# Attention and a tiled feed-forward on one core: weights placed beside x, sums on GpSimd, low-rank factors from the preamble, row-tiled low-rank products

## The chip, the cores and the metric

One core of one Trainium2 chip runs the whole program. The metric is the device time of one launch in microseconds. TensorE (PE; its weight loads are PEld), VectorE (DVE), ScalarE (ACT), GpSimd (POOL) and SyncE (SP, which only issues DMAs) each run their own list of instructions in order and wait for one another through semaphores.

## What is computed

T = 2048 tokens of 512 features; 128 heads of 4 content and 64 rope features; a feed-forward with 1376 hidden rows. `tile` repeats a matrix of 128 columns four times.

```python
def _L0_attn_ref(x, Wq_down, Wq_up, Wq_rope, Wkv_down, Wk_up, Wv_up, Wk_rope, Wo):
    ...
    scores = (jnp.einsum('bqhd,bkhd->bhqk', q_c, k_c) + jnp.einsum('bqhd,bkd->bhqk', q_r, k_r)) / scale
    attn = jax.nn.softmax(scores, axis=-1)
    out = jnp.einsum('bhqk,bkhd->bqhd', attn, v_c)
    ...
    return out @ Wo
def _qlora_linear(x, wq, A, B):
    w = jnp.tile(wq, (1, 4))
    return x @ w.T + x @ A.T @ B.T * 0.5
def _L0_ffn_ref(x, ...):
    gate = jax.nn.silu(_qlora_linear(x, w1q, a1, b1))
    up = _qlora_linear(x, w3q, a3, b3)
    return _qlora_linear(gate * up, w2q, a2, b2)
xn = _layernorm(x, axis=-1)
s = attention(xn)
g = _silu(_L0_ffn_ref(xn, ...))
return x + s * g
```

## The kernel before

**Precision.** A float32 product is made of three passes of reduced operands: high by high, low by high and high by low. ScalarE copies a value to the reduced type (the high part, names in `h`), and VectorE or GpSimd subtracts it from the original (the low part, names in `l`). A product written with plain float32 operands takes one instruction in the program, but the trace counts two or more passes for it.

**Preamble** (`project_inputs`, 0 to 77 us). It normalises x, transposes it into `xh` and `xl` (4 blocks of 128 features by 2048 tokens each, resident to the end), and projects it by the columns of `ws`: 128 columns of latents, 64 of the key's rope part (`kp`, rows 0 to 63) and the same 64 once more, whose high part ScalarE puts in `krlh` rows 64 to 127. What SyncE stores last ends it.

**Attention** (`attention`, 77 to 1805 us). `groups` runs `body` of each engine over 16 groups of 16 steps, in a rolled loop; the last group is unrolled. A step projects one block of queries (`project`), makes row scores by query block for the maxima (`row_scores`), and two steps later the scores with keys in the rows (`scores`), the exponentials, and the values. For each pair of steps VectorE's maxima are transposed and laid by a SyncE DMA (`max_rows`, `slot<-mrow`) into the row of the operand that subtracts them; the scores wait for it. In the unrolled last group, each engine runs `tail(eng, k)` of `finish` behind `body(at, k)`, for steps k = 0 to 22 (16 and above finish what the first 16 began). SyncE's order in a step is contents (`slot<-kc`, `k<-kc`), maxima row, values, stores of the outputs.

**Feed-forward** (`finish`). Since `tile` repeats the weights, x can be summed over its four blocks first: `sums` has TensorE multiply `xh` and `xl` by ones-on-the-diagonal (`oner`), 8 products for each of four chunks of 512 tokens, in the tail at k = 17 and 19; the results are split into `sh` and `sl`. `lora` then makes the low-rank products x A of all chunks (`lah`, `lal`: the factors three times over), 48 products, split into `lr`. A chunk (`tensor_rest`, `chunk`) has 12 column tiles of hidden rows (three row ranges `FR` = 128, 128, 88 of each of four blocks of 344): each tile makes `gp` and `up` from 3 weight products and 1 low-rank product (`b13` by `lr`, 96 rows) each, L1384 to L1387. ScalarE applies Silu, VectorE multiplies (`hid`, L1268), adds the blocks (`hsum`, L1280) and splits the sum; after tiles 5 and 9 and after the loop `low_rank` (L1355) multiplies `hid` by `a2` into `zp`, four products in four column strips. Beside it the attention output of the chunk is loaded (`num`, `den`), VectorE takes reciprocals of `den` (L1245, one for each of four feature blocks, in the y stage), GpSimd multiplies (`normalise`, L1098), and both parts of the result go to `attn_out` (L1369, 12 products for 128 tokens). The y stage makes for each 128 tokens 9 products of hidden sums by `w2h`, `w2l` (L1409) and one of `z` by `b2` in float32 (L1411), applies Silu, multiplies by the attention output and adds x. In chunk 0, `weights_hi` splits w2 and Wo between the tiles. Chunks 1 and 2 run in a rolled loop.

## Time and profile before

| | us |
|---|---|
| median of the runs (2024.77 to 2025.87) | 2024.78 |
| the profiled execution | 2028.5 |
| its span | 2026.4 |
| TensorE busy | 1984.1 |
| VectorE busy | 1411.8 |
| ScalarE busy | 1060.0 |
| GpSimd busy | 468.2 |
| chain that ended last: TensorE's share | 93% |

The profiled execution is one launch; its span is from the first to the last instruction of the trace, and all times in the rows below are in it. Busy times of engines overlap. Matmuls are pipelined, so the difference between two starts, and not a row's duration, is what one costs. A matmul in float32 shows as x2 or more.

### The profile page before, as it was taken

The numbers are of one execution on the slowest core, as the hardware profiler recorded it, in microseconds if no ns is written. First come the engines' busy times: TensorE is split into PE (matmuls) and PEld (weight loads), VectorE is DVE, ScalarE is ACT, GpSimd is POOL, SyncE is SP. The second block draws the span as 40 slices with busy tenths as digits, with TensorE's granted clock in tenths as the row PEclk, the third lists the DMA queues.
The fourth block names the chain that finished last, engine by engine and source line by source line (L and its number), as shares of the span: only waits on it lengthen the run. The fifth ranks groups of instructions, "written<-read, shape, count | busy, mean of one in ns | idle before, by whom it ended". The sixth has DMA issues, their size and how long they took to land.

```text
span 2026.4 us, 38967 instructions
## 1 busy us (share of the span) xinstructions
PE 1984.1 (98%) x12576; PEld 1532.0 (76%) x12576; DVE 1411.8 (70%) x1619; ACT 1060.0 (52%) x1539; POOL 468.2 (23%) x771
## 2 busy tenths in 40 slices
PE   7799999999999999999999999999999999988998
PEld 5577777777777777777777777777777777866776
DVE  7667667677676676776767767667677676767664
ACT  5355555555555555555555555555555555553222
POOL 2112121212222222212121212121212222114221
PEclk9899999999999999999999999999999999999999
DMA  7412121211112121212121212111111112122221
GB/s 253 149 28 43 34 40 38 39 35 38 39 32 44 28 47 29 49 28 48 26 49 28 49 29 42 33 39 38 39 35 38 39 32 63 26 77 89 84 83 47
DMA packets 128856, 102.69 MB, mean 51 GB/s; under 512 B 51510, under 2 KB 94518, under 8 KB 128814
## 3 DMA queue, kind: packets, MB, share of 16 engines
q1 hardware_dynamic: 128814, 102.15, 21.5%
q8 instruction: 24, 0.39, 0.1%
q14 instruction: 18, 0.15, 0.0%
HBM read 50.71 MB, written 25.17 MB: 37 GB/s over the span
## 4 chain that ended last, share of the span: by engine, by line
PE 93%; DVE 2%; ACT 1%; issue 1%; POOLq 0%; ACTq 0%; DVEq 0%
PE pj L879 35%; PE st L849 24%; PE sx L866 12%; PE ob L826 12%; PE ap L1369 2%; PE sx L834 1%; PE zp L1409 1%; PE yp L1409 1%; PE gp L1384 1%; PE zp L1355 1%; PE up L1387 0%; PE gp L1387 0%; PE up L1386 0%; PE gp L1385 0%; PE up L1384 0%
## 5 line engine op out<-in xcount | busy, mean ns | idle before, releaser
L785 DVE TENSOR_REDUCE mx<-sx 128x4 f32<-128x1024 f32 x512 | 627.0, 1225 | 452.9 <-PE sx L866 434.8
L766 ACT ACTIVATE probs<-st 128x1024 f32<-128x1024 f32 x512 | 512.7, 1026 | 166.6 <-PE st L849 166.6
L736 ACT ACTIVATE slot<-pj 64x512 fp32r<-64x512 f32 x512 | 303.9, 594 | 443.5 <-PE pj L879 437.2
L849 PE MATMUL st<-slot,k 89*128 89x512 f32 x1024 | 417.8, 408 | 1.2 <-ACT probs L766 1.2
L686 POOL CAST k<-kc 64x512 fp32r<-64x512 f32 x256 | 167.4, 654 | 1060.4 <-PE st L849 1060.1
L849 PE MATMUL st<-slot,krlh 128*128 128x512 f32 x1024 | 406.9, 397 | 0.0
L879 PE MATMUL pj<-xh,wh 128*128 128x512 f32 x1024 | 402.6, 393 | 4.0 <-PEq L216 3.0
L879 PE MATMUL pj<-xh,wl 128*128 128x512 f32 x1024 | 402.2, 393 | 0.0
L879 PE MATMUL pj<-xl,wh 128*128 128x512 f32 x1024 | 402.0, 393 | 0.0
L795 DVE TENSOR_TENSOR slot<-pj,slot 64x512 fp32r<-64x512 f32 x512 | 352.7, 689 | 16.3 <-ACT slot L736 0.3
L866 PEld LDWEIGHTS sx<-k,slot 88*128 88x128 f32 x2048 | 306.8, 190 | 66.8 <-issue 28.4
L866 PE MATMUL sx<-k,slot 88*128 88x256 f32 x2048 | 335.4, 286 | 4.4 <-DVE mx L785 2.7
L826 PE MATMUL ob<-probs,vx 128*32 128x256 f32 x4096 | 247.6, 382 | 0.0
L879 PEld LDWEIGHTS pj<-xh,wh 128*128 128x128 f32 x1024 | 193.9, 189 | 42.4 <-issue 5.0
L879 PEld LDWEIGHTS pj<-xh,wl 128*128 128x128 f32 x1024 | 193.5, 189 | 42.0
L879 PEld LDWEIGHTS pj<-xl,wh 128*128 128x128 f32 x1024 | 193.8, 189 | 38.0
L849 PEld LDWEIGHTS st<-slot,k 89*128 89x128 f32 x1024 | 195.6, 191 | 30.5 <-issue 2.2
L849 PEld LDWEIGHTS st<-slot,krlh 128*128 128x128 f32 x1024 | 195.1, 191 | 29.4
L826 PEld LDWEIGHTS ob<-probs,vx 128*32 128x32 f32 x4096 | 120.0, 109 | 83.4 <-issue 0.4
L799 DVE CAST slot<-slot 64x1024 fp32r<-64x1024 f32 x256 | 176.0, 688 | 7.9
L719 POOL TENSOR_TENSOR wl<-w_stage,wh 128x512 fp32r<-128x512 f32 x60 | 77.0, 1283 | 59.1 <-ACT wh L771 59.1
L747 ACT ACTIVATE mrow<-sx 16x128 fp32r<-16x128 f32 x128 | 33.3, 260 | 86.1 <-PE sx L834 86.1
(168 smaller groups left out, 1405.5 us busy)
## 6 DMA issues: line engine op xcount, KB each, us to landing
w_stage<-in_Wq_rope SPq DMA_DIRECT2D x64, 256.0 KB, 3.0
c_scratch<-stage SPq DMA_DIRECT2D x32, 256.0 KB, 2.9
c_in<-c_scratch SPq DMA_DIRECT2D x128, 64.0 KB, 1.9
o_scratch<-o_sb SPq DMA_DIRECT2D x128, 64.0 KB, 2.1
k<-kc SPq DMA_DIRECT2D x128, 48.0 KB
slot<-kc SPq DMA_DIRECT2D x256, 24.0 KB
k<-kx SPq DMA_DIRECT2D x128, 48.0 KB
slot<-kx SPq DMA_DIRECT2D x256, 24.0 KB
```

The lines of the kernel that those rows point to most:

```text
L686: nc.gpsimd.tensor_copy(k1[0:64, s, :, :].rearrange("p a n -> p (a n)"), krh[:, bp * CH:(bp + 1) * CH]).then_inc(k_ready, 1)
L719: nc.gpsimd.tensor_tensor(wl[:, s], w_stage[:, s % 2], wh[:, s], ALU.subtract).then_inc(w_ready, 1)
L736: nc.scalar.activation(slot1[0:64, (k - 1) % NS, e, :, :], pj[64 * e:64 * e + 64, :].rearrange("p (a n) -> p a n", a=2), ACT.Copy).then_in ...
L766: nc.scalar.activation(probs[:, k % NS, kt], st[:, kt], ACT.Exp, scale=SCALE).then_inc(exp_done, 1)
L785: nc.vector.tensor_reduce(mx[:, p, lo:lo + 4], sx[:, :, :].rearrange("p a (b k) -> p (a b) k", b=2), axis=AX.X, op=ALU.max).then_inc(red_d ...
L795: nc.vector.tensor_tensor(slot2[64:128, s, e, :, :], pj[64 * e:64 * e + 64, :].rearrange("p (a n) -> p a n", a=2), slot1[0:64, s, e, :, :] ...
L799: nc.vector.tensor_copy(slot2[0:64, s], slot1[0:64, s]).then_inc(s2_done, 1)
L826: last = nc.tensor.matmul(ob[j:j + 32, 0, :], vx[:, s, 2 * h + kt, e, :], probs[:, s, kt, h, e * S:(e + 1) * S], start=(s == 0 and kt == 0 ...
L849: last = nc.tensor.matmul(st[:, kt, h, :].rearrange("p (e n) -> p e n", e=PH), kk, q[0:n_rows, s, :, h, :], start=(n == 0), stop=(n == 1))
L866: last = nc.tensor.matmul(sx[:, h, qt * S:(qt + 1) * S], slot1[0:KC, s, half, h, qt * 128:qt * 128 + 128], k1[0:KC, s, h, :], start=True, ...
L879: last = nc.tensor.matmul(pj[:, :], w[:, s, c, :], xx[:, c, ts], start=(c == 0 and n == 0), stop=(c == KD - 1 and n == 2))
L1369: last = nc.tensor.matmul(ap[i % 2][:, :], o[:, k, i * 128:(i + 1) * 128], w[:, k, :], start=(k == 0 and n == 0), stop=(k == KD - 1 and n ...
```

## The change

**Preamble.** The second copy of the key's 64 columns in `ws` gives way to the low-rank factors: `a1T` and `a3T` are loaded, GpSimd clears the columns and copies the factors in six times, so that rows 64 to 127 of `kp` hold x A; ScalarE puts them in `lora_raw`. ScalarE splits `ws` in two pieces. What was the second copy now comes by a DMA from `krh` to `krlh` in each chunk.

**Tail of the last group.** The sums over the four blocks of x are made by GpSimd in float32, 28 additions, at most two in a step (k below 16). The weights are loaded into the space of x's low parts of groups that are done (`x_raw`, which shares memory with `xl`), and their high and low parts into slices of `xh` and `xl`; ScalarE and VectorE split them between the steps. The low-rank factors b come in 42 DMAs of two partitions at k = 2; masks (`mk`, made at k = 0) choose for each partition whether it holds the high or the low part, so that 12 rows of one operand carry all three terms. Half of the reciprocals are taken at k = 15 and 16, on `den1`, which holds the denominator of each head once and is spread to its rows through a scratch in memory by broadcast DMAs.

**Feed-forward.** No sums and no low-rank products stand ahead of it. 11 column tiles replace 12: the remainders of 88 rows carry a piece of the fourth block in rows 96 and up (a second VectorE product in these tiles). A tile has six `wide` products and two `narrow` ones (rows 32g to 32g + 11 of `b13` and of `lora`, in one of four row strips by `tile_position`). The narrow ones of two tiles stand together. `z` by `b2` is one reduced product whose rows carry three terms (`zh` by ScalarE, `zt` and `z` by VectorE). One reciprocal in a chunk stands behind column tile 7. TensorE's chunks are unrolled.

```diff
-            sp.dma_start(ws[:, :, 192:256], wk_rope.rearrange("(k p) n -> p k n", p=128)).then_inc(small_loaded, 16)
+            for n, a in enumerate((a1T, a3T)):
+                sp.dma_start(a_raw[:, :, RANK * n:RANK * (n + 1)],
+                             a.rearrange("(k p) n -> p k n", p=128)).then_inc(a_loaded, 16)
...
+                sp.wait_ge(krh_done, c + 1)
+                sp.dma_start(krlh[64:128, c * CH:(c + 1) * CH].bitcast(F32),
+                             krh[:, c * CH:(c + 1) * CH].bitcast(F32)).then_inc(krh_copied, 16)
...
+            nc.gpsimd.memset(ws[:, :, 192:256], 0.0).then_inc(a_zero, 1)
+            pool.wait_ge(a_zero, 1)
+            pool.wait_ge(a_loaded, 32)
+            for g in range(2):
+                for n in range(3):
+                    lo = 192 + 32 * g + 2 * RANK * n
+                    nc.gpsimd.tensor_copy(ws[:, :, lo:lo + 2 * RANK], a_raw[:, :, :]).then_inc(a_copied, 1)
+            pool.wait_ge(ws_hi, 2)
...
-                nc.scalar.activation(krlh[64:128, xs], kp[64:128, :], ACT.Copy).then_inc(krh_done, 1)
+                nc.scalar.activation(lora_raw[:, xs], kp[64:128, :], ACT.Copy).then_inc(lora_done, 1)
...
-            act.wait_ge(small_loaded, 64)
-            nc.scalar.activation(wsh[:, :, :], ws[:, :, :], ACT.Copy).then_inc(ws_hi, 1)
+            act.wait_ge(small_loaded, 48)
+            nc.scalar.activation(wsh[:, :, 0:128], ws[:, :, 0:128], ACT.Copy).then_inc(ws_hi, 1)
             for i in range(NTL):
                 hi_transposed(0, i)
+                if i == 1:
+                    act.wait_ge(a_copied, 6)
+                    nc.scalar.activation(wsh[:, :, 128:256], ws[:, :, 128:256], ACT.Copy).then_inc(ws_hi, 1)
...
+    def spread_den(sp):
+
+        for kt in range(KD):
+            sp.dma_start(den[:, kt, :], r_dram[32 * kt:32 * kt + 32, :].unsqueeze(1).broadcast_to([32, HD, CH])
+                         ).then_inc(den_spread, 16)
...
     def sync_tail(sp, k):
-        if k == 5:
...
-        if k == 16:
+        if k == 2:
+            sp.wait_ge(b_zero, 1)
+            for g in range(4):
+                w, half = g // 2, g % 2
+                for n in range(3):
+                    r = 32 * g + 4 * n + 2 * w
+                    for jj in range(2):
+                        j = 2 * jj + half
+                        src = (b1T, b3T)[w]
+                        if j < 3:
+                            sp.dma_start(b13_raw[r:r + RANK, jj * 384:jj * 384 + FB],
+                                         src[:, j * FB:(j + 1) * FB]).then_inc(b_loaded, 16)
+                            sp.dma_start(b13_raw[r:r + RANK, jj * 384 + 352:jj * 384 + 352 + PIECE[j]],
+                                         src[:, 3 * FB + 256 + 32 * j:3 * FB + 256 + 32 * j + PIECE[j]]).then_inc(b_loaded, 16)
+                        else:
+                            sp.dma_start(b13_raw[r:r + RANK, jj * 384:jj * 384 + 256],
+                                         src[:, j * FB:j * FB + 256]).then_inc(b_loaded, 16)
...
+        if k == 13:
+            sp.wait_ge(at_sems.proj_done, projected(11))
+            sp.wait_ge(s_step, 21)
+            sp.dma_start(wo_raw, wo.rearrange("(k p) n -> p k n", p=128)).then_inc(wo_loaded, 16)
+        if k == 17:
             for landed in at_sems.ct_in:
                 sp.wait_ge(landed, 48 * NT)
-            sp.wait_ge(at_sems.o_stored, 32 * (NT - 2))
-            load_attention(sp, o_dram, den, 1, 0, den_loaded)
...
+        if k == 18:
+            sp.wait_ge(ab2_zero, 2)
+            sp.wait_ge(r_stored, 16)
+            spread_den(sp)
+            load_num(sp, 0)
+            sp.dma_start(w2_raw[:, 0:2, :], w2qT[0:256, :].rearrange("(k p) n -> p k n", p=128)).then_inc(w2_loaded, 16)
+            sp.dma_start(w2_raw[0:FR[2], 2, :], w2qT[256:FB, :]).then_inc(w2_loaded, 16)
+            for r in range(NR):
+                sp.dma_start(a2[0:FR[r], r, :, 0:RANK],
+                             a2T.rearrange("(j p) n -> p j n", j=4)[128 * r:128 * r + FR[r], :, :]).then_inc(a2_loaded, 16)
+            for j in range(4):
+                for n in range(3):
+                    sp.dma_start(b2_raw[32 * j + RANK * n:32 * j + RANK * (n + 1), :], b2T).then_inc(b2_loaded, 16)
 
...
     def pool_tail(pool, k):
...
+        if k == 1:
+            nc.gpsimd.memset(b13_raw[:, :], 0.0).then_inc(b_zero, 1)
+        if k < 16:
+            cs = slice(c * CH, (c + 1) * CH)
+            terms = [xx[:, kt, cs] for kt in range(KD) for xx in (xh, xl)]
+            for n in range(2 * (k % 4), min(2 * (k % 4) + 2, 7)):
+                if n:
+                    pool.wait_ge(s_step, 7 * c + n)
+                nc.gpsimd.tensor_tensor(s_raw[:, cs], s_raw[:, cs] if n else terms[0], terms[n + 1],
+                                        ALU.add).then_inc(s_step, 1)
+        if k in (4, 8):
+            w = c - 1
+            pool.wait_ge(at_sems.proj_done, projected(4 * w + 3))
+            pool.wait_ge(s_step, 7 * w + 7)
+            nc.gpsimd.memset(x_raw[:, :, w * CH + FB:w * CH + 384], 0.0).then_inc(pad_zero, 1)
+        if k == 16:
+            pool.wait_ge(at_sems.proj_done, projected(15))
+            pool.wait_ge(s_step, 28)
+            nc.gpsimd.memset(a2[:, :, :, :], 0.0).then_inc(ab2_zero, 1)
+            nc.gpsimd.memset(b2_raw, 0.0).then_inc(ab2_zero, 1)
...
     def act_tail(act, k):
...
+        if k in (4, 6, 8):
+            i = k // 2 - 2
+            act.wait_ge(b_loaded, 16 * 42)
+            wait(act, b_done, i)
+            nc.scalar.activation(b13_hi[:, :], b13_raw[:, 256 * i:256 * i + 256], ACT.Copy, scale=0.5).then_inc(b_hi_done, 1)
...
     def vector_tail(dve, k):
...
+        if k in (6, 10, 14, 18):
+            c = k // 4 - 1
+            cs = slice(c * CH, (c + 1) * CH)
+            dve.wait_ge(sh_done, c + 1)
+            nc.vector.tensor_tensor(sl[:, cs], s_raw[:, cs], sh[:, cs], ALU.subtract).then_inc(sl_done, 1)
...
+        if k in (15, 16):
+            n = k - 15
+            dve.wait_ge(den_loaded, 16)
+            nc.vector.reciprocal(den1[:, 256 * n:256 * n + 256], den1[:, 256 * n:256 * n + 256]).then_inc(recip, 1)
...
                     wait(dve, zmm_done, c * NR + max(r - 1, 0))
-                nc.vector.tensor_tensor(hid[0:n, r % 2, j, :], up[m % 2][0:n, :], gate[0:n, m % 2, :],
-                                        ALU.mult).then_inc(hid_done, 1)
+                product = nc.vector.tensor_tensor(hid[0:n, r % 2, j, :], up[m % 2][0:n, :], gate[0:n, m % 2, :], ALU.mult)
+                if r == 2:
+                    lo = 32 * j
+                    product = nc.vector.tensor_tensor(hid[lo:lo + PIECE[j], 0, 3, :], up[m % 2][96:96 + PIECE[j], :],
+                                                      gate[96:96 + PIECE[j], m % 2, :], ALU.mult)
+                product.then_inc(hid_done, 1)
                 if j == 1 and r > 0:
                     lo_part(c, r - 1)
...
                                             ALU.subtract).then_inc(ol_done, 1)
+                if m == 7 and more:
+                    dve.wait_ge(den_loaded, 16 * (c + 2))
+                    nc.vector.reciprocal(den1[:, :], den1[:, :]).then_inc(recip, 1)
...
+            add_block(c, 2, 3)
+            lo_part(c, 2)
+            dve.wait_ge(zh_done, c + 1)
+            wait(dve, z_done, c)
+            nc.vector.tensor_scalar(zt[:, :], zp[:, :], mk[:, 4:5], None, ALU.mult).then_inc(zt_done, 1)
+            dve.wait_ge(zt_done, c + 1)
+            wait(dve, y_done, c * NI)
+            nc.vector.scalar_tensor_tensor(out=z[:, :], in0=zh[:, :], scalar=mk[:, 5:6], in1=zt[:, :],
+                                           op0=ALU.mult, op1=ALU.add).then_inc(z_done, 1)
             for i in range(NI):
...
     def tensor_tail(pe, k):
-        if k == 17:
-            pe.wait_ge(la_hi, 1)
-            pe.wait_ge(at_sems.ql_done, 2 * NS * NT)
-            sums(pe, 0)
-            pe.wait_ge(at_sems.red_done, 2 * NS * NT)
-            sums(pe, 1)
-        if k == 19:
-            pe.wait_ge(at_sems.mrow_ready, NS * NT // 2)
-            sums(pe, 2)
...
-            sums(pe, 3)
-
...
     def tensor_rest(pe):
-        def lora(c):
-            if c < NC - 1:
-                pe.wait_ge(sl_done, c + 2)
-            else:
-                pe.wait_ge(lr_done, 1)
-            for k in range(KD):
-                for n, (w, xx) in enumerate(((lah, xh), (lah, xl), (lal, xh))):
-                    last = nc.tensor.matmul(tb[(NC + c) % 3][0:96, :], w[:, k, :], xx[:, k, c * CH:(c + 1) * CH],
-                                            start=(k == 0 and n == 0), stop=(k == KD - 1 and n == 2))
-            last.then_inc(lp_done, 1)
...
+            def wide(m):
+
+                r, j = m // 4, m % 4
+                for w, (dst, done) in enumerate(banks):
+                    wide_h, wide_l = (x[:, j, w * CH + 128 * r:w * CH + 128 * r + 128] for x in (xh, xl))
+                    nc.tensor.matmul(dst[m % 2][:, :], wide_h, sh[:, cs], start=(m % 2 == 0), stop=False)
+                    nc.tensor.matmul(dst[m % 2][:, :], wide_h, sl[:, cs], start=False, stop=False)
+                    last = nc.tensor.matmul(dst[m % 2][:, :], wide_l, sh[:, cs], start=False, stop=(m % 2 == 1))
+                    if m % 2:
+                        last.then_inc(done, 1)
+
+            def narrow(m):
+
+                r, j = m // 4, m % 4
+                for w, (dst, done) in enumerate(banks):
+                    row = 32 * (2 * w + j % 2)
+                    lo = 384 * (j // 2) + 128 * r
+                    last = nc.tensor.matmul(dst[m % 2][:, :], b13[row:row + LR, lo:lo + 128], lora[row:row + LR, cs],
+                                            start=(m % 2 == 1), stop=(m % 2 == 0), tile_position=(row, 0))
+                    if m % 2 == 0:
+                        last.then_inc(done, 1)
+
+            def bank_free(m):
+                if m >= 2:
+                    pe.wait_ge(hid_done, c * MT + m - 1)
+                else:
+                    wait(pe, hid_done, c * MT)
...
+            for m in range(0, MT, 2):
+                bank_free(m)
+                wide(m)
+                if m + 1 < MT:
+                    bank_free(m + 1)
+                narrow(m)
+                if m + 1 < MT:
+                    narrow(m + 1)
+                    wide(m + 1)
+                if m in (4, 8):
+                    low_rank(m // 4 - 1)
...
                         nc.tensor.matmul(yp[i % 2][:, :], h[0:n, r, ts], w[0:n, r, :],
                                          start=(r == 0 and q == 0), stop=False)
-                nc.tensor.matmul(yp[i % 2][:, :], z[:, ts], b2[:, :], start=False, stop=True).then_inc(y_done, 1)
```

Three places of the order in which the engines run.

SyncE, in the last group around step 2 (`slot1<-mrow`: the row of maxima; `k1<-kc`, `slot1<-kc`: contents). Before:

```order
L622 DMA slot1<-kc 12x1x512 x2
L618 DMA k1<-kc 24x1x512
L622 DMA slot1<-kc 12x1x512 x2
L653 DMA o_scratch<-o_sb 64x256 x2
L628 DMA slot1<-mrow 1x16x128
L618 DMA k1<-kc 24x1x512
```

Now, with 38 further DMAs of the same kind, two partitions each, where "..." stands:

```order
L647 DMA slot1<-kc 12x1x512 x2
L678 DMA o_scratch<-o_sb 64x256 x2
L1074 DMA b13_raw<-in_b1T 2x344
L1076 DMA b13_raw<-in_b1T 2x32
...
L1076 DMA b13_raw<-in_b3T 2x32
L1079 DMA b13_raw<-in_b3T 2x256
L653 DMA slot1<-mrow 1x16x128
L643 DMA k1<-kc 24x1x512
L647 DMA slot1<-kc 12x1x512 x2
```

42 DMAs of the factors b now stand between the store of an output and the row of maxima of step 0, and so ahead of the contents of step 3 too.

TensorE, the first column tiles of a chunk (`gp`, `up`: the banks of gate and up; 0 and 1 alternate with the tiles). Before:

```order
L1384 MATMUL gp0<-sh,w13h 128x512
L1385 MATMUL gp0<-sl,w13h 128x512
L1386 MATMUL gp0<-sh,w13l 128x512
L1387 MATMUL gp0<-lr,b13 128x512
L1384 MATMUL up0<-sh,w13h 128x512
L1385 MATMUL up0<-sl,w13h 128x512
L1386 MATMUL up0<-sh,w13l 128x512
L1387 MATMUL up0<-lr,b13 128x512
L1384 MATMUL gp1<-sh,w13h 128x512
```

Now (`kx` is the memory of `lora`):

```order
L1427 MATMUL gp0<-sh,xh 128x512
L1428 MATMUL gp0<-sl,xh 128x512
L1429 MATMUL gp0<-sh,xl 128x512
L1427 MATMUL up0<-sh,xh 128x512
L1428 MATMUL up0<-sl,xh 128x512
L1429 MATMUL up0<-sh,xl 128x512
L1439 MATMUL gp0<-kx,b13 128x512
L1439 MATMUL up0<-kx,b13 128x512
L1439 MATMUL gp1<-kx,b13 128x512
L1439 MATMUL up1<-kx,b13 128x512
L1427 MATMUL gp1<-sh,xh 128x512
L1428 MATMUL gp1<-sl,xh 128x512
```

The two low-rank products of each tile have moved out of its eight and stand with those of the next tile, four in a row.

VectorE, from column tile 7 on in a chunk with a next one. Before (its four reciprocals stand further on, in the y stage):

```order
L1268 TENSOR_TENSOR hid<-up1,gate 128x512
L1276 REGISTER_ALU
L1280 TENSOR_TENSOR hsum<-hsum,hid 128x512
L1264 REGISTER_ALU
L1268 TENSOR_TENSOR hid<-up0,gate 88x512
L1264 REGISTER_ALU
L1268 TENSOR_TENSOR hid<-up1,gate 88x512
```

Now:

```order
L1372 TENSOR_TENSOR hid<-up1,gate 128x512
L1345 REGISTER_ALU
L1349 TENSOR_TENSOR hsum<-hsum,hid 128x512
L1389 ISA
L1390 RECIPROCAL den1<-den1 128x512
L1368 REGISTER_ALU
L1372 TENSOR_TENSOR hid<-up0,gate 88x512
L1375 TENSOR_TENSOR hid<-up0,gate 32x512
L1368 REGISTER_ALU
L1372 TENSOR_TENSOR hid<-up1,gate 88x512
L1375 TENSOR_TENSOR hid<-up1,gate 32x512
```

The reciprocal stands ahead of the products of tiles 8 and 9, which have each become two, and the y stage keeps none.

## Rows read from the trace of the kernel before

**Rows 1.** Busy line of the page: busy us, share of the span, instructions.

```profile
PE 1984.1 (98%) x12576; PEld 1532.0 (76%) x12576; DVE 1411.8 (70%) x1619; ACT 1060.0 (52%) x1539; POOL 468.2 (23%) x771
```

**Rows 2.** Stretches: us, length, busy us (x instructions) of PE, PEld, DVE, ACT, POOL; PEclk, DMA share, GB/s.

```profile
150.00:1780.00 1630.00, 1630.00 (x10917) 1274.11 (x10916) 1147.43 (x1287) 902.77 (x1285) 377.28 (x681) 1.00 0.19 38
1874.90:1923.49 48.59, 48.59 (x214) 34.59 (x212) 34.26 (x36) 14.14 (x24) 10.16 (x9) 1.00 0.26 87
1817.44:1874.90 57.46, 49.20 (x214) 34.33 (x212) 41.98 (x37) 20.75 (x32) 26.74 (x16) 1.00 0.32 99
76.00:82.00 6.00, 5.22 (x12) 3.80 (x12) 4.23 (x5) 0.00 (x0) 3.63 (x7) 0.50 0.50 161
```

**Rows 3.** Chain that ended last, two chunks' first output products: start us, us, what.

```profile
1903.72 2.95 PE ap L1369 x12
...
1952.31 2.95 PE ap L1369 x12
```

**Rows 4.** Timeline of PE: start us, us, engine, line, operation, out<-in, count.

```profile
1882.52 0.40 PE L1384 MATMUL gp<-sh,w13h 128*128 x1
...
1884.39 0.39 PE L1384 MATMUL gp<-sh,w13h 128*128 x1
...
1886.04 0.39 PE L1387 MATMUL up<-lr,b 96*128 x1
1886.35 1.06 PE L1355 MATMUL zp<-hid,a 128*32 128x512 f32 x8
1887.35 0.51 PE L1384 MATMUL gp<-sh,w13h 128*128 x1
1887.69 0.40 PE L1385 MATMUL gp<-sl,w13h 128*128 x1
```

**Rows 5.** Timeline of PE in the y stage.

```profile
1868.57 1.02 PE L1411 MATMUL yp<-b,z 128*128 128x512 f32 x2
...
1869.66 0.39 PE L1369 MATMUL ap<-wol,xh 128*128 128x512 f32 x1
```

**Rows 6.** Timeline of GpSimd and VectorE in chunk 0.

```profile
1830.50 2.85 POOL L1123 TENSOR_TENSOR w2l<-raw,w2h 128x1024 fp32r<-128x1024 f32 x1
...
1831.02 2.89 DVE L1285 TENSOR_TENSOR xl<-num,xh 128x512 fp32r<-128x512 f32 x1
...
1833.83 0.68 DVE L1268 TENSOR_TENSOR hid<-up,gate 128x512 f32<-128x512 f32 x1
...
1854.23 3.34 DVE L1245 RECIPROCAL den<-den 128x512 f32<-128x512 f32 x1
```

**Rows 7.** Timeline of PE, from the first low-rank product to the first gate product.

```profile
1804.74 0.48 PE L1338 MATMUL tb<-xh,lah 128*96 128x512 f32 x1
...
1817.44 0.39 PE L1384 MATMUL gp<-sh,w13h 128*128 128x512 f32 x1
```

**Rows 8.** Issues of DMAs: count, KB each, us to landing.

```profile
slot<-mrow SPq DMA_DIRECT2D x128, 8.0 KB, 1.8
```

**Rows 9.** Groups of the page: count, busy us, mean ns, idle before and releaser.

```profile
L785 DVE TENSOR_REDUCE mx<-sx 128x4 f32<-128x1024 f32 x512 | 627.0, 1225 | 452.9 <-PE sx L866 434.8
...
L766 ACT ACTIVATE probs<-st 128x1024 f32<-128x1024 f32 x512 | 512.7, 1026 | 166.6 <-PE st L849 166.6
...
L719 POOL TENSOR_TENSOR wl<-w_stage,wh 128x512 fp32r<-128x512 f32 x60 | 77.0, 1283 | 59.1 <-ACT wh L771 59.1
```

**Rows 10.** Timeline of SyncE's queue in the last group.

```profile
1691.43 1.19 SPq L653 DMA_DIRECT2D o_scratch<-o_sb  x2
1696.38 0.57 SPq L628 DMA_DIRECT2D slot<-mrow  x1
...
1801.14 0.25 SPq L1025 DMA_DIRECT2D rawb<-in_b1T  x1
1801.44 0.25 SPq L1026 DMA_DIRECT2D rawb<-in_b3T  x1
```

**Rows 11.** Timeline of PE: the first score that needs the row of maxima.

```profile
1700.45 0.40 PE L849 MATMUL st<-slot,k 89*128 89x512 f32 x1
```

**Rows 12.** The loads of a2: duration ns min/median/max, first and last start.

```profile
L1038 SPq DMA_DIRECT2D a<-in_a2T x3: 390/508/3020, 1814.3 to 1815.3; - x3
```

506 lines of the change are left out of this document (240 added, 266 removed).

## The prediction, as recorded before the result

> **What bounds the kernel now.** I read the page's busy line first, then stretches of time, then the instructions inside them. TensorE is busy 98% of the span [rows 1], and through the attention (150 to 1780 us) it is busy every microsecond at a granted clock of 1.00 [rows 2]: there only TensorE's work counts, and everything else has room until it makes TensorE wait. The edit changes that program in its last sixteen steps alone, and what comes behind. The feed-forward has four chunks of 512 tokens. The steady ones repeat every 48.59 us (attention-output products at 1903.72 and at 1952.31, [rows 3]) with TensorE busy for all 48.59 us and VectorE for 34.26 [rows 2]. The first chunk takes 57.46 us, 8.9 more, TensorE being busy for only 49.20 of them [rows 2]. So the end is TensorE's count of products plus whatever makes it wait.
>
> **The products, chunk by chunk.** A column tile (eight products) starts at 1882.52 and the next at 1884.39: 1.87 us, 0.2335 a product [rows 4]. Twelve tiles make 22.4 us. The new loop has 11 tiles with six wide products each, 66 x 0.2335 = 15.4 us, and six groups of "narrow" products (12 rows in one of four row strips). No row shows a row-strip product. Its bounds: free concurrency and no changeover, 0.23 us a group; four in series, 0.93. The nearest row is the low-rank group, four f32 products in four column strips. From 1886.27 (where the next product would have stood) to 1887.35, plus the 0.11 by which the next spacing (0.34) is long [rows 4], it costs 1.19 us, while one f32 product alone costs 1869.66 - 1868.57 - 0.23 = 0.86 [rows 5]. So a group costs one product plus 0.33 of changeover: I take 0.23 + 0.33 = 0.56, six times 3.4. The loop's products fall from 22.4 to 18.8, by 3.6. The y products: the last of ten (z by b2) was f32 at 0.86 and becomes a single pass at 0.23, four times 0.63 = 2.5. TensorE's floor in a chunk is 48.6 - 3.6 - 2.5 = 42.5 us.
>
> The Trainium skill (TensorE: Matmul & The Clock Gate, Measured speedup vs the span model) has four row tiles at 3.07 times, and (TensorEngine Tiling (Array Packing), Key Properties) says that changing the tiling mode drains the engine. By the first alone a group would be 0.30 us and the four chunks some 6 us shorter; by the second there is a changeover on top, and the low-rank rows [rows 4] agree with it.
>
> **VectorE becomes the limit inside the loop.** Its 32 short operations of a steady chunk average (34.26 - 4 x 3.34)/32 = 0.65 us [rows 2, 6]. Of the four reciprocals one is left, but it moves from the y stage into the loop, behind column tile 7. From the end of tile 7 VectorE does product, add, reciprocal 3.34, then the two parts of product 8: 0.2 + 4 x 0.67 + 3.34 = 6.2 us. TensorE needs product 8 for tile 10, and until there has 1.4 (wide 8) + 0.56 + 1.4 (wide 9) + 1.2 (low rank) = 4.5: it waits some 1.8. Tiles 3 to 6 hold twelve VectorE operations (7.8 us) against 6.7 us of TensorE, and part of that arrears, 0.5, comes out at tile 8. So chunks 1 and 2 take 42.5 + 2.3 = 44.8; the last one has no reciprocal, 42.5 + 0.3 = 42.8. Gains: 3.8, 3.8 and 5.8. The z chain (ScalarE, then two VectorE operations in a row, about 2.5 us) lies beside twelve attention-output products (2.73 us) and costs nothing by a hair; if that cover were gone it would be 0.5 a chunk.
>
> Chunk 0 loses its wait for the b factors (8.9 over the steady length, before) but has new work on the same queues: w2's low part, b2's two masking operations, and on ScalarE a wait for twelve b2 loads queued behind 2.7 MB (1.0 of spread denominators, 1.0 of outputs, 0.7 of w2). The extra lies between 0 and the old 8.9; I take 3.4: chunk 0 is 48.2, a gain of 9.3.
>
> **From the end of attention to the first tile.** The 48 low-rank products and their wait, 1804.74 to 1817.44, go: 12.7 us [rows 7]. The 32 sum products go, two blocks of 16 x 0.2335 = 3.7 us; they covered waits. The first block lay over the landing of the row of maxima (1.8 us [rows 8]), the second over an exponential (1.03 us [rows 9]) and its handoffs. I let 3.1 of the 7.5 come back as waiting, between 0 and 7.5. GpSimd's sums end two steps earlier and the weights' splitting at step 18, so nothing later is due; VectorE's second half-reciprocal pushes the last maxima by under 1 us, which is in the 3.1. Gain 17.1.
>
> **What is added in the attention's last group.** (a) SyncE: 42 DMAs at step 2, each of two partitions. Two in a row of this kind start 0.295 us apart [rows 10], so they hold the queue for 12.4 us. Behind them stands the row of maxima for step 0 and the contents of step 3. In the old order the queue is idle from 1692.62 to 1696.38, 3.8 us, and the maxima land at 1696.38 + 1.8 = 1698.2, needed at 1700.45 [rows 8, 10, 11]. So TensorE stops for 12.4 - 3.8 - 2.2 = 6.4 us, and 0.6 more for the contents two DMAs further: 7.0. Nothing hides it, as every score waits for that row. After a pause of this size the clock may fall: at 76 to 82 us the clock reads 0.50, the lower level of 1.2 GHz, behind waits at the end of the preamble [rows 2], where twelve products at half the clock cost 12 x 0.23 = 2.8 us more; in chunk 0, with 8.3 us of pauses, it stayed 1.00. I take 1.5. (b) VectorE's, ScalarE's and GpSimd's extra pieces. VectorE idles before the first maxima of each step (452.9 us over 256 steps, 1.8 each [rows 9]), and the pieces are up to 2.8 us (step 6). GpSimd adds 28 sums of 1.28 us, two a step (the 128x512 difference in [rows 9]). Such an instruction can hold up a VectorE operation with two SBUF inputs: in chunk 0 the difference, whose kind takes 0.68 us, that starts at 1831.02 took 2.89 and ended 0.6 after GpSimd's 1830.50 + 2.85 [rows 6]. Few of VectorE's operations in the steps have two SBUF inputs, so I take 1.0 for the sixteen steps, bounds 0 and 20 (below). (c) Preamble: two small loads, a later split of half the weights, a 64-partition copy per chunk on SyncE, whose queue ends the preamble: 0.5.
>
> **Sum.** -9.3 -3.8 -3.8 -5.8 -17.1 + 7.0 + 1.5 + 1.0 + 0.5 = -29.8. The profiled execution took 2028.5 (span 2026.4); the median of the runs is 2024.8, and the same difference is taken off it: **1995 us**.
>
> **Rivals.**
> A. The 42 DMAs do not stop TensorE, since they may issue faster when nothing else is queued: without 7.0 + 1.5 it is 1986.5. Against it: the rows of such DMAs agree within 0.01. 12%.
> B. The strips do not overlap or cost two changeovers, 0.93 instead of 0.56: 6 x 0.37 = 2.2 less a part hidden by the VectorE waits, about 1.8 a chunk, and chunk 0 keeps 3 more: 2005. 17%.
> C. GpSimd's sums hold VectorE in each of the sixteen steps for one instruction, 1.28 us, with no room left: 16 x 1.28 = 20, 2015. For it: the 2.89 us row. Against it: VectorE's casts and maxima stood beside GpSimd's work unchanged so far. 11%. The Trainium skill (GPSIMD Engine Reference, Specifications) says that GpSimd contends with VectorE operations that have two SBUF inputs or run in a 2-port mode; the second half of that would add the casts of the steps to those held, and is what C would need.
> D. Slower than before: a two-partition DMA costs not 0.3 but 1.2 us at step 2. The stop is then 42 x 1.2 - 5.4 = 45 us, 2024.8 - 38.3 + 45 + 1.5 = 2033. It decides from 1.0 us a DMA, (38.3 - 1.5 + 5.4)/42. For it: one a2 load took 3.02 us to issue [rows 12], behind outputs and w2, 1.7 MB; against it, step 2 has next to nothing queued. 5%.
> E. The end is set elsewhere by a new wait of some 30 us that I don't see: no change, 3%.
> The forecast keeps 52%.
>
> **How the numbers follow.** The range takes in A, B and the unknowns of the forecast (chunk 0 by -3 to +5, the sums by 3) and most of C's way: 1983 to 2011, leaving out C's upper part, D and E. About 0.2% is what a measurement can tell from no change. Faster 0.92, same 0.03, slower 0.05.
>
> **What would show it.** One pause of TensorE of about 7 us near 1700, waiting for the maxima's row; the first gate product near 1810 (1817.4 - 17.1 + 10.0), with no low-rank product ahead of it; chunk starts 48, then 45 and 45 apart; in each of the first three chunks a wait of about 2 us on the product of tile 8 behind the reciprocal; four narrow products starting within 0.1 us of each other. It would be wrong if the steps with sums are longer than 6.7 us throughout, or the narrow products start 0.23 apart.

## The result

The changed kernel takes 2012.9 us (median of four, 2012.7 to 2014.1) against 2025.0 for the kernel before on the same chip: a ratio of 0.994 (95% interval 0.992 to 0.996). It is faster, but by 12 us, where 30 were forecast, and above the upper end of the range. The profiled execution's span fell from 2026.4 to 2011.0, by 15.4. The execution profiled before was 3.7 us longer than the median of its runs (2028.5 and 2024.8), so some 3 us of the difference between 12 and 15 very likely belong to it alone. It came to the last group 2.3 us later (projection of step 2 at 1690.50, now 1688.19), although both traces have the same projection at 147.4 and 147.5: its steps in the rolled loop were longer by 0.01 us each. Why is open, since one trace of that kernel is all there is. On other chips the kernel before was between 2023.5 and 2031.4, so that the experiments are read by their stages first and by ratios second.

Engines of the changed kernel, as [rows 1]:

```profile
PE 1949.5 (97%) x12448; PEld 1502.3 (75%) x12448; DVE 1403.3 (70%) x1654; ACT 1051.1 (52%) x1535; POOL 491.6 (24%) x798
```

The forecast was 48.2 us for the first chunk, 44.8 for the second and third, and 5.8 less than before for the last. These are the four chunks, from first gate product to first gate product and to the end (columns as in [rows 2]):

```profile
1810.31:1867.06 56.75, 46.89 (x204) 31.32 (x201) 29.68 (x40) 15.14 (x28) 15.51 (x13) 0.91 0.40 116
1867.06:1915.99 48.93, 46.34 (x201) 31.56 (x200) 27.44 (x37) 12.98 (x23) 10.13 (x8) 0.93 0.31 97
1915.99:1962.04 46.05, 43.45 (x201) 29.53 (x200) 27.45 (x37) 12.86 (x23) 10.14 (x8) 1.00 0.32 103
1962.04:2011.00 48.96, 43.27 (x201) 29.38 (x199) 25.05 (x37) 13.46 (x24) 6.41 (x5) 0.99 0.13 49
```

Before they were 57.2, 48.6, 48.6 and 54.5 (first gate products at 1817.44, 1874.68, 1923.28 and 1971.87; the 57.46 of [rows 2] ends 0.2 later). Only the last one gained what was forecast (5.6; forecast 5.8). The first gained 0.5 (9.3), the second lost 0.3 (a gain of 3.8), the third gained 2.5 (3.8). TensorE's own work is near the forecast of 42.5: it is busy for 43.3 us in the last chunk. The rest is waiting, and a clock of 0.91 and 0.93 in the first two.

In the attention's last group, the queue of SyncE, as [rows 10]; TensorE behind it:

```profile
1690.73 0.26 SPq L1074 DMA_DIRECT2D b_raw<-in_b1T  x1
...
1703.05 0.25 SPq L1079 DMA_DIRECT2D b_raw<-in_b3T  x1
1703.42 0.58 SPq L653 DMA_DIRECT2D slot<-mrow  x1
```

```profile
1705.32 0.79 PE L874 MATMUL st<-slot,k 89*128 89x512 f32 x1 [6.51 <-DMA slot<-mrow]
```

The 42 loads run from 1690.73 to 1703.30, 12.6 us, the row of maxima leaves behind them, and TensorE stands 6.51 us. That step takes 15.19 us in place of 6.59. The step before it takes 7.14 in place of 6.74, but not for the queue: TensorE waits 0.38 us for VectorE's maxima there, which stand behind two masks. Further on, first projections of three steps in a row:

```profile
1723.81 0.40 PE L904 MATMUL pj<-xh,wh 128*128 128x512 f32 x1
...
1731.57 0.47 PE L904 MATMUL pj<-xh,wh 128*128 128x512 f32 x1
...
1739.26 0.39 PE L904 MATMUL pj<-xh,wh 128*128 128x512 f32 x1
```

The two steps between them take 7.76 and 7.69 us (before 6.74 and 6.59), and so do two more at 1753 to 1768: 4.2 us in all, 4.6 with the 0.4 of step 2. VectorE and GpSimd at that place:

```profile
1726.50 0.72 DVE L1299 TENSOR_SCALAR lora_raw<-lora_raw,mk 64x512 f32<-64x512 f32 x1
1727.26 0.98 DVE L1301 SCALAR_TENSOR_TENSOR kx<-lora_hi,mk,lora_raw 64x512 fp32r<-64x512 f32 x1
1728.16 0.69 DVE L1315 TENSOR_TENSOR sl<-s_raw,sh 128x512 fp32r<-128x512 f32 x1
...
1731.46 2.54 DVE L824 CAST slot<-slot 64x1024 fp32r<-64x1024 f32 x1
```

```profile
1730.05 1.29 POOL L1163 TENSOR_TENSOR s_raw<-s_raw,xh 128x512 f32<-128x512 f32 x1
...
1732.15 1.30 POOL L1163 TENSOR_TENSOR s_raw<-s_raw,xl 128x512 f32<-128x512 f32 x1
```

The cast of the queries (`slot<-slot`) takes 2.54 us here. In the last group before the change all of them took 0.68 to 0.70. It starts just behind one of GpSimd's additions (1730.05 + 1.29) and ends 0.55 us behind the next (1732.15 + 1.30). It is the picture of [rows 6] with a cast that has one input. Of the 16 casts of the last group, two took 2.54 us and three 1.86 to 1.88.

In chunk 0: SyncE's queue; GpSimd's first multiplication; ScalarE; the third column tile:

```profile
1801.05 0.57 SPq L1104 DMA_DIRECT2D r_scratch<-den  x1
...
1805.86 2.91 SPq L1054 DMA_DIRECT2D den<-r_scratch  x4
1808.81 2.62 SPq L1059 DMA_DIRECT2D num<-o_scratch  x4
1811.48 0.86 SPq L1110 DMA_DIRECT2D x_raw<-in_w2qT  x1
```

```profile
1819.96 4.93 POOL L1181 TENSOR_TENSOR num<-num,den 128x512 f32<-128x512 f32 x4 [19.79 <-DMA num<-o_scratch]
```

```profile
1821.86 1.06 ACT L1239 ACTIVATE xh<-x_raw 128x1024 fp32r<-128x1024 f32 x1 [7.92 <-DMA x_raw<-in_w2qT]
```

```profile
1824.69 0.80 PE L1427 MATMUL gp<-sh,xh 128*128 128x512 f32 x1 [7.22 <-DVE hid L1372]
```

The reciprocals go to memory at 1801.05 and come back by broadcasts from 1805.86 on; outputs and w2 stand behind. GpSimd stood idle for 19.79 us until 1819.96, ScalarE for 7.92 until 1821.86, and TensorE for 7.22. It then ran at half the clock until 1832.

In chunk 1, the first wide product of tile 10, the stretch behind it, and the same place and stretch in chunk 2:

```profile
1889.49 0.50 PE L1427 MATMUL gp<-sh,xh 128*128 128x512 f32 x1 [2.23 <-DVE hid L1375]
...
1938.41 0.50 PE L1427 MATMUL gp<-sh,xh 128*128 128x512 f32 x1 [2.23 <-DVE hid L1375]
```

```profile
1889.50:1896.50 7.00, 7.00 (x18) 4.78 (x19) 5.49 (x8) 0.93 (x2) 0.00 (x0) 0.55 0.60 190
1936.00:1942.00 6.00, 3.77 (x19) 2.55 (x16) 5.78 (x8) 0.60 (x1) 0.00 (x0) 1.00 0.32 109
```

The wait for VectorE is 2.23 us in both (forecast 1.8). Behind it the granted clock is 0.55 for 7 us in chunk 1, the lower level of 1.2 GHz for nearly all of it, and 1.00 in chunk 2. The chunks differ by 2.9 us.

### The profile page after: what moved, and what is told of

Its sections match the earlier page's. It is cut to its first block, busy times and chain, and to the rows that moved or that the text cites. A ratio compares the mean times of both kernels' runs of the same rounds, so it can differ in the third digit from the quotient of the medians.

```text
span 2011.0 us, 38744 instructions
## 1 busy us (share of the span) xinstructions
PE 1949.5 (97%) x12448; PEld 1502.3 (75%) x12448; DVE 1403.3 (70%) x1654; ACT 1051.1 (52%) x1535; POOL 491.6 (24%) x798
## 4 chain that ended last, share of the span: by engine, by line
PE 90%; DVE 3%; SPq 1%; issue 1%; DMA 1%; ACT 1%; POOLq 0%; DVEq 0%; ACTq 0%
PE pj L904 34%; PE st L874 23%; PE sx L891 12%; PE ob L851 11%; PE ap L1473 2%; PE sx L859 1%; PE yp L1506 1%; PE zp L1506 1%; PE gp L1427 1%; DVE mx L810 1%; PE gp L1439 0%; DMA x_raw<-in_w2qT 0%; PE zp L1459 0%; DVE hid L1372 0%; PE up L1429 0%
## 5 line engine op out<-in xcount | busy, mean ns | idle before, releaser
L824 DVE CAST slot<-slot 64x1024 fp32r<-64x1024 f32 x256 | 183.2, 716 | 8.0
```

Of the source, the lines that this page charges most:

```text
L824: nc.vector.tensor_copy(slot2[0:64, s], slot1[0:64, s]).then_inc(s2_done, 1)
```

## Experiments

### The 42 loads spread over four steps

```diff
-        if k == 2:
+        if k in (2, 3, 4, 5):
...
+            cut = (0, 11, 20, 32, 42)
+            for r, lo, n, src, at in pieces[cut[k - 2]:cut[k - 1]]:
```

> The changed kernel with its 42 loads of the factors b spread over four steps (11, 9, 12 and 10 of them at k = 2, 3, 4, 5) in place of all at k = 2; the splits of b come two steps later (ScalarE at 6, 8, 10, VectorE at 7, 9, 11). Theory (the queue): behind the 42 loads the row of maxima left at 1703.42 in place of some 1694, TensorE stood 6.51 us at 1705 and ran at half the clock for a while after; two steps were 9.1 us over their 6.65. Spread, 12 loads take 3.5 us, which the queue has idle, so 9.1 goes: 2012.9 - 9.1 = 2003.8. Rival (a load costs its place wherever it stands, since every row of maxima has a slack of only 2.2 us): four shorter pauses, sum 4 or more left, 2008 or over.

Measured 2008.4, ratio 0.990 (0.988 to 0.992). The two steps are 7.15 and 6.66 in place of 7.14 and 15.19, and no other step grew by more than 0.4: 8.1 us less from step 2 to step 15. So the stop is the queue's, and spread loads show no price of their own. The 7.15 stays, so it is not the queue's. The time is 4.6 above what this theory gave. In the profiled execution chunk 0 starts at 1803.27, 7 us earlier, and takes 57.7, and both chunk 1 and chunk 2 have the half clock (48.9 each; chunk 2 was 46.05). Whether the earlier start brought the second half clock is not shown: it comes and goes in the unchanged kernel too (below).

### GpSimd's additions left out

```diff
+                if n == 0:
+                    nc.gpsimd.tensor_tensor(s_raw[:, cs], terms[0], terms[1], ALU.add).then_inc(s_step, 1)
+                else:
+                    nc.gpsimd.sem_inc(s_step, 1)
```

> The changed kernel with 24 of GpSimd's 28 additions left out (the first of each seven stays, so the sums over x are wrong). Theory (GpSimd's additions hold VectorE's casts, which then hold the row maxima, where VectorE has extra pieces): the cast of 2.54 us in the slow steps is 0.69 again, and the four steps of 7.7 us are 6.7, 4.1 us in all, about 2009. Rival (VectorE's own pieces are too long in these steps, two masks of a low-rank factor, the low part of a sum and a content's low part): the steps stay at 7.3 us or over, 2011 or more.

The pairs of slow steps are 7.76 and 6.66, and 7.68 and 6.70. One of each pair healed and one stayed: both theories are half right. TensorE and VectorE there:

```profile
1733.05 0.28 PE L859 MATMUL sx<-ident,mx 128*16 128x128 f32 x1 [0.96 <-DVE mx L810]
```

```profile
1734.46 1.12 DVE L824 CAST slot<-slot 64x1024 fp32r<-64x1024 f32 x1
...
1740.76 1.87 DVE L824 CAST slot<-slot 64x1024 fp32r<-64x1024 f32 x1
```

The first slow step is made by the wait of 0.96 us (1.00 in the changed kernel). It ends before either cast starts and no addition stands beside it, so it is VectorE's own pieces (2.4 us of masks and the low part of a sum, in a step that also splits contents). The second step healed when its cast fell from 2.54 to 1.12, so it came from GpSimd's additions. The 1.12 is still long, beside GpSimd's cast of keys. The cast beside the addition that was left takes 1.87 and costs no step its length. The time, 2014.2 beside 2013.8 for the unchanged kernel, does not show the 2 us. In this trace step 2 of the last group came 3.6 us later than in the unchanged kernel's, chunk 0 took 58.3, and four executions scatter by 3 us.

### The changed kernel once more, beside others

> The changed kernel itself, unchanged, on the chip and in the rounds of the three kernels beside it, since the kernel before moved by 3 us from chip to chip. Every theory expects 2012 to 2015, and in its trace the stop of 8.5 us at the third step, two pairs of steps at 7.7 us, the pause of 7 us in chunk 0, and a half clock behind one or two of the pauses of 2.2 us in chunks 1 and 2, not always the same ones.

2013.8 (ratio 0.994, 0.992 to 0.996), with the stop (15.42), the slow steps, chunk 0 at 55.8, chunk 1 at 48.9 and chunk 2 at 47.4, chunk 2 with 3 us of half clock this time. So the clock behind the pauses of 2.2 us is not the same in every execution. Some pauses are followed by a half clock and some are not.

### w2 early

> The changed kernel with the two loads of w2 issued at k = 16, ahead of the last row of maxima, in place of behind the spread denominators and the outputs at k = 18. Theory 1 (w2 alone is what chunk 0 waits for): the pause of 7.2 us at the third column tile and the 3 us that the half clock costs behind it go, about 2003. Theory 2 (everything behind the store of the reciprocals is late: the outputs, for which GpSimd starts only at 1819.96, and b2, for which ScalarE waits again at 1824.59): ScalarE then waits for these, the pause only shrinks by what 0.7 MB take in the queues, 2 to 4 us, with the clock still falling: 2009 to 2011.

2009.1 (0.991, 0.989 to 0.993). ScalarE and TensorE:

```profile
1819.99 0.63 ACT L1246 ACTIVATE zh<-x_raw 128x512 fp32r<-128x512 f32 x1 [3.16 <-DMA x_raw<-in_b2T]
```

```profile
1822.46 0.79 PE L1442 MATMUL gp<-kx,b 12*128 12x512 f32 x1 [3.21 <-DVE hid L1375]
```

ScalarE no longer waits for w2, but then for b2 (3.16 us), and TensorE waits 3.21 us one tile later. Chunk 0 is 53.1 in place of 55.8 to 56.8. Theory 2 holds: w2 was only the last of several.

### Outputs ahead of the round trip

```diff
...
             sp.dma_start(r_dram[:, :], den1[:, :]).then_inc(r_stored, 16)
+            load_num(sp, 0)
...
```

> As the run with w2 early, and besides the loads of the outputs stand ahead of the wait for the stored reciprocals, and ScalarE's and VectorE's splits of b2 come at tile 6 in place of tiles 2 and 3. Theory 2 (order of the loads): ScalarE waits for nothing longer than a microsecond, the pause of 7.2 us and the half clock after it (3 us) go: 2002 to 2004, with chunk 0 at 47 to 49 us in place of 56.75. Rival (the loads are bound by their 2.7 MB, whatever the order): GpSimd's first multiplication still starts near 1818, and 3 us or more of pause are left, 2007 or over.

2014.0 (0.993, 0.991 to 0.994): nothing gained, chunk 0 took 57.7. ScalarE:

```profile
1813.86 0.38 ACT L768 ACTIVATE o_sb<-ob 128x256 f32<-128x256 f32 x1 [3.97 <-DMA o_scratch<-o_sb]
```

The store of an attention output was queued behind the four loads (1804.89 in place of 1801.74). ScalarE's last copy waits for its landing, and the first gate waits behind that copy. Both theories had left this out. The order was changed once more, with the outputs behind that store:

> The changed kernel with w2's loads at k = 16, the outputs' loads at k = 18 ahead of the wait for the stored reciprocals but behind the last stores of outputs of the attention, a2 and b2 last, and the splits of b2 at tile 6. In the earlier order ScalarE stood 3.97 us in front of its last copy of an attention output, since the store ahead had been issued 3.2 us later, behind four loads. Theory (the order alone decides, and that store was what fell late): no wait of ScalarE over 1 us in chunk 0, no pause over 2.5 us of TensorE ahead of tile 10, chunk 0 at 47 to 50 us in place of 56.75: 6 to 9 below the changed kernel. Rival (the spread of the reciprocals, 1 MB behind a round trip of 4.8 us, is too late in any order): GpSimd starts after 1816, two or more us of pause stay at tiles 3 or 4, and chunk 0 stays over 52.

2012.7 (0.994, 0.991 to 0.996), chunk 0 at 54.7. The wait for the store is gone, and what is left is the rival's:

```profile
1819.24 6.00 POOL L1184 TENSOR_TENSOR num<-num,den 128x512 f32<-128x512 f32 x4 [18.69 <-DMA den<-r_scratch]
```

GpSimd waits for the spread reciprocals until 1819.24, although they were issued between 1807.55 and 1810.3, and ScalarE waits 3.74 us for GpSimd. None of the three orders heals chunk 0: the round trip through memory with 1 MB of broadcast behind it is too late in each.

### The reciprocal moved to the y stage

```diff
-                if m == 7 and more:
-                    dve.wait_ge(den_loaded, 16 * (c + 2))
-                    nc.vector.reciprocal(den1[:, :], den1[:, :]).then_inc(recip, 1)
...
+            if more:
+                dve.wait_ge(den_loaded, 16 * (c + 2))
+                nc.vector.reciprocal(den1[:, :], den1[:, :]).then_inc(recip, 1)
             for i in range(NI):
```

> The changed kernel with the reciprocal of a chunk moved from behind column tile 7 to the y stage, behind the two operations that make z (SyncE loads the next outputs ahead of waiting for it). Theory: the three pauses at tile 10 (2.14, 2.23, 2.23 us) go, and the half clock of 1890 to 1897 in chunk 1, which began behind one of them and makes chunk 1 longer than chunk 2 by 2.9, goes too: 2012.9 - 6.6 - 2.9 = 2003.4. Rival 1 (the clock falls for what chunk 0 did, not for this pause): 2006.3. Rival 2 (the 3.34 us hold up the y stage or the next chunk's outputs instead): 2011 or over.

2010.9 (0.992, 0.989 to 0.994). The pauses at tile 10 are gone, but the next chunk has one at its third tile, in chunks 1, 2 and 3 (2.95, 2.07, 1.93 us). GpSimd got the spread reciprocals only at 1862.23, after 35.88 us of idleness, so the outputs were late:

```profile
1862.23 1.29 POOL L1181 TENSOR_TENSOR num<-num,den 128x512 f32<-128x512 f32 x1 [35.88 <-DMA den<-r_scratch]
```

```profile
1870.84 0.50 PE L1427 MATMUL gp<-sh,xh 128*128 128x512 f32 x1 [2.95 <-DVE hid L1372]
```

The half clock followed these pauses in chunks 2 and 3, and chunks 1 to 3 took 46.6, 47.1 and 52.5 us in place of 48.9, 46.05 and 49.0. Rival 2 holds. With one reciprocal and a round trip both places that were tried cost time: it is too long in the loop and too late in the y stage.

### Four reciprocals, as before the change

```diff
-                load_den(sp, c + 1)
-                hold(sp, passed, recip, c + 3)
-                hold(sp, passed, den_spread, (c + 1) * 16 * KD)
-                sp.dma_start(r_dram[:, :], den1[:, :]).then_inc(r_stored, 16)
                 hold(sp, passed, ol_done, (c + 1) * KD)
+                load_attention(sp, o_dram, den, 1, c + 1, den_spread)
                 load_num(sp, c + 1)
-                hold(sp, passed, r_stored, 16 * (c + 2))
-                spread_den(sp)
...
+                    nc.vector.reciprocal(den[:, i, :], den[:, i, :]).then_inc(recip4, 1)
...
```

> The changed kernel with the denominators of chunks 1 to 3 treated as before the change: four loads of the spread-out denominators, four reciprocals of VectorE in the y stage, no store and no broadcast. Theory (one reciprocal in the loop is dearer than four in the y stage, where VectorE has time and GpSimd can follow piece by piece): the pauses of 2.1 to 2.2 us at tile 10 go in three chunks, none comes in their place, and no half clock follows: chunks 1 and 2 are 43 to 44 us, 9 us off the changed kernel in all. Rival (TensorE's shorter y stage no longer covers 13.4 us of reciprocals, so that the next outputs are late): a pause of 1 us or more at the third tile of the next chunk, chunks 1 and 2 over 45.

2002.4 (0.988, 0.987 to 0.990), 11.4 below the unchanged kernel beside it. Its chunks 0 and 1:

```profile
1810.81:1865.31 54.50, 46.71 (x205) 31.37 (x201) 39.13 (x43) 15.15 (x28) 14.30 (x12) 0.91 0.36 108
1865.31:1908.88 43.57, 43.18 (x201) 29.54 (x200) 36.98 (x41) 12.88 (x23) 10.18 (x8) 1.00 0.29 97
```

Chunks 1 and 2 are 43.6, TensorE is busy for 43.2 of them at a full clock, with VectorE at 37.0 in place of 27.4. VectorE takes four reciprocals in place of one, and the three more cost nothing in the y stage. Against the trace of the unchanged kernel beside it, undoing this one part gains 1.3 us in chunk 0 (54.5 for 55.8), 5.3 in chunk 1 and 3.8 in chunk 2: 10.4 of the 11.4.

### Chunk 0 as before too

> All reciprocals as before the change, chunk 0 too: its four loads of spread-out denominators at k = 16, the reciprocals at k = 17 to 20, Wo's low part on GpSimd at k = 17 and 18, no scratch; w2's loads at k = 16, b2's split at tile 6. Theory (chunk 0's pause was GpSimd waiting for a broadcast that landed 9 to 12 us after it was issued, behind a round trip): GpSimd's first multiplication starts before 1812 in place of 1819, no pause of TensorE over 1.5 us in chunk 0, no half clock behind it, chunk 0 at 46 to 48.5 in place of 54.5: 2002.4 - 7 = 1995. Rival (1 MB of outputs that land late, or VectorE's 13.4 us of reciprocals that reach into the first tiles): chunk 0 at 50 or over, 1998 or more.

2000.7 (0.986, 0.985 to 0.988). Chunk 0 is 49.2 in place of 54.5, a little above the 46 to 48.5 expected. The early loads of w2 and the later split of b2, which this run has too, were in the run above that stayed at 54.7, so what healed chunk 0 should be that the round trip is gone. One doubt is left. GpSimd's first multiplication starts at 1815.20 and not before 1812, and that is ahead of the first gate product only because this came at 1817.28 instead of 1810.8, which gave the loads time. The last run below has no such delay and settles it. SyncE and TensorE at the end of the attention:

```profile
1793.24 2.61 SPq L116 DMA_DIRECT2D den<-o_scratch  x4
...
1796.59 0.42 SPq L1106 DMA_DIRECT2D x_raw<-in_w2qT  x1
1801.82 0.60 SPq L653 DMA_DIRECT2D slot<-mrow  x1
```

```profile
1806.78 0.79 PE L874 MATMUL st<-slot,k 89*128 89x512 f32 x1 [4.50 <-DMA slot<-mrow]
```

The last row of maxima leaves 5 us behind 1.7 MB of loads and lands late: TensorE waits 4.50 us and starts again at half the clock. From the projection of step 15 to the first gate product it is 27.0 us in place of 22.2. That took back most of what chunk 0 gave, and I had not counted it.

### Pieces moved off the busy steps

> The changed kernel with the 42 loads of b spread over k = 2 to 5, and VectorE's extra pieces moved off the steps in which it also splits contents (k = 2, 6, 10, 14): masks of the low-rank factors at 3, 5, 7, 9, of b at 8, 11, 13, low parts of the sums at 8, 12, 15, 18, of w1 and w3 at 11 to 14 (ScalarE's parts shifted to match). With fewer sums, one of each pair of slow steps stayed at 7.7 us and the other fell to 6.7. Theory (both VectorE's pieces and GpSimd's additions are needed to pass its slack, so moving the pieces away heals both): no step over 6.9, last projection some 13 us earlier than in the changed kernel at the same start (8.7 of the stop and 4.5 of the steps), 2000 to 2001. Rival (GpSimd's additions hold the casts wherever the pieces stand): steps of 7.5 and more stay, 2003 or over.

2007.1 (0.991, 0.989 to 0.992). From the projection of step 2 to that of step 15 it is 89.2 us, before the change 86.8, in the changed kernel 100.0. The four slow steps and the half slow one are down to two, of 7.68 and 7.58. In the first the cast takes 2.56 us again, with 1.2 us of mask behind it. In the second it is a mask of b that is held:

```profile
1763.31 0.85 DVE L1309 TENSOR_SCALAR b_raw<-b_raw,mk 128x256 f32<-128x256 f32 x1
1764.20 1.46 DVE L1311 SCALAR_TENSOR_TENSOR b<-b_hi,mk,b_raw 128x256 fp32r<-128x256 f32 x1
```

At 1729.53 in this run the same two took 0.34 and 0.48 with no addition beside them; here two additions of GpSimd stand beside them (1762.73 and 1764.09), and with a low part of w3 they make 3.3 us in one step. So both steps that stayed have a hold by GpSimd with a further piece in the same step. Moving the pieces healed two of the four, and of the rival's signs both came: steps over 7.5, and a time over 2003. The time is 6 above the expectation: chunk 0 now pauses for 8.22 us and runs at half the clock for about 8 us. It starts 10 us earlier and waits for the same loads.

### Narrow products in twos

```diff
...
+                narrow(m)
                 if m + 1 < MT:
                     bank_free(m + 1)
-                narrow(m)
-                if m + 1 < MT:
-                    narrow(m + 1)
                     wide(m + 1)
+                    narrow(m + 1)
```

> The kernel with the denominators of chunks 1 to 3 as before (2002.4, where nothing but TensorE bounds the tiles of chunks 1 to 3), with the two narrow products of each tile behind its own six wide ones: eleven groups of two in place of five groups of four and one of two, the same products. Theory (a group costs one product, 0.23, and a changeover of 0.30 us, whatever is in it): five more groups of 0.53 in a chunk, 2.6 us longer each, 10 in all, 2012. Rival (no changeover, four strips at once are worth what two are): the chunks stay within 0.5 us, 2002 to 2004.

2011.7 (0.992, 0.990 to 0.993), 9 above the kernel it was made from (2002.4, in other rounds on another chip, where the kernel before was 1.7 faster; by spans the four chunks together are 7.2 longer). In four and in two; the changed kernel first:

```profile
1868.20 0.39 PE L1429 MATMUL up<-sh,xl 128*128 128x512 f32 x1
...
1868.53 0.50 PE L1439 MATMUL up<-kx,b 12*128 12x512 f32 x1
...
1868.96 0.50 PE L1427 MATMUL gp<-sh,xh 128*128 128x512 f32 x1
1869.30 0.39 PE L1428 MATMUL gp<-sl,xh 128*128 128x512 f32 x1
```

```profile
1870.63 0.39 PE L1428 MATMUL up<-sh,xl 128*128 128x512 f32 x1
1870.94 0.50 PE L1436 MATMUL gp<-kx,b 12*128 12x512 f32 x1
...
1871.37 0.50 PE L1426 MATMUL gp<-sh,xh 128*128 128x512 f32 x1
1871.71 0.39 PE L1427 MATMUL gp<-sl,xh 128*128 128x512 f32 x1
```

```profile
1869.49:1914.97 45.48, 45.48 (x202) 30.41 (x201) 37.03 (x41) 13.20 (x23) 10.18 (x8) 1.00 0.27 93
```

Four start within 0.01 us, and from the product ahead of them to the one behind them it takes 0.76, of which 0.23 is the product ahead: 0.53 the group. Two take 0.51. The product behind a group is longer too, 0.34 in place of 0.23 to the next start; with that a group of four costs 0.64 and a group of two 0.62. A chunk is 45.5 in place of 43.6. TensorE's busy time grew from 43.2 to 45.5, since the wait of 0.4 at tile 9 is gone: 2.3 us for five more groups, 0.46 each, where 0.53 was expected. The price is the changeover, and two products more in a group are nearly free.

### Together

> The two kernels beside it together: loads of b spread, VectorE's pieces moved, all reciprocals as before the change, w2 early. Theory (the costs are apart and add up): 13 us at the steps and 18 in the chunks off the changed kernel, 2013.8 - 13 - 18 = 1983, 1.9 to 2.2% below the kernel before. Rival (what is saved at the steps is given back in chunk 0, whose loads then start earlier against the same stores, or half clocks show up elsewhere): 1988 or over.

1986.2 (1985.3 to 1990.2), ratio 0.979 (0.978 to 0.981): faster than both kernels, between what the theory gave (1983) and the rival's 1988. Its chunks 0 and 1, and GpSimd's first multiplication:

```profile
1803.64:1852.35 48.71, 44.72 (x204) 30.48 (x201) 42.57 (x44) 14.96 (x28) 15.34 (x12) 0.96 0.25 81
1852.35:1895.92 43.57, 43.20 (x201) 29.54 (x200) 36.97 (x41) 12.88 (x23) 10.19 (x8) 1.00 0.28 97
```

```profile
1806.46 5.98 POOL L1185 TENSOR_TENSOR num<-num,den 128x512 f32<-128x512 f32 x4 [13.95 <-DMA num<-o_scratch]
```

The steps take 89.2 us in place of 100.0, chunk 0 48.7 in place of 56.8, chunks 1 and 2 43.6 in place of 48.9 and 46.0. GpSimd starts 2.8 us behind the first gate product (at 1803.64), where in the changed kernel it was 9.6 us, so chunk 0 is healed without a late start. By spans 22.6 us are gained on the changed kernel: the steps, chunk 0 and chunks 1 and 2 give 26.7, and 2.7 go back between step 15 and the first gate product (24.8 for 22.1) and 1.5 in a later start of the last group. The gains add up because most of the pauses, and with them most of the half clock, are gone: the mean clock is 0.96 in chunk 0, where pauses of 2.51 and 1.48 us are left, and 1.00 in chunks 1 and 2. The wait for the last row of maxima is 1.52 here and not 4.50, with the same loads ahead, since the row leaves 7 us behind them.

## Why the prediction was wrong, point by point

By spans the forecast was 2026.4 - 29.8 = 1996.6, and 2011.0 was measured: 14.4 us are to be found.

| term | forecast | measured | missing |
|---|---|---|---|
| chunk 0 | -9.3 | -0.5 | 8.8 |
| chunk 1 | -3.8 | +0.3 | 4.1 |
| chunk 2 | -3.8 | -2.5 | 1.3 |
| chunk 3 | -5.8 | -5.6 | 0.2 |
| end of attention | -17.1 | -18.0 | -0.9 |
| stop behind the loads, with the clock | +8.5 | +8.6 | 0.1 |
| VectorE's and GpSimd's pieces | +1.0 | +4.6 | 3.6 |
| up to the last group | +0.5 | -2.3 | -2.8 |

The last row is probably the profiled execution of before, as said above. The first gate product came at 1810.31, where "near 1810" was forecast. The two largest terms up to there, -17.1 and +8.5, were right one by one; that the sum agrees to 0.1 us is luck, since the 3.6 that the pieces cost more was made up by the 2.8 of the last row and 0.9 at the end of the attention. Most of what fell is in the chunks.

**Chunk 0 is the step that failed.** I had bounded its extra work "between 0 and the old 8.9", as one term of 3.4, for w2, b2 and a wait of ScalarE. The round trip of the reciprocals (store, landing, four broadcasts) was in the diff and in no term. The bound was taken from the old kernel's wait, although the new one has another chain. In the changed kernel chunk 0's 56.75 us are 43.2 of work, 9.9 of pauses (the longest 7.22) and some 3.6 of half clock; the forecast had 42.5, 2.3 and 3.4. The runs showed the cause: no order of the loads brought chunk 0 under 53, and without the round trip it was 49.2 and 48.7. That is near the forecast's 48.2, for a kernel that does not have this part.

The old wait was misread as well. The prediction put it all down to the factors b, but of the old chunk 0's four pauses (3.16, 1.32, 2.46, 1.31 us) only the first stands behind ScalarE's split of b (and a load of its function table):

```profile
1824.48 0.50 PE L1384 MATMUL gp<-sh,w13h 128*128 128x512 f32 x1 [3.16 <-DVE hid L1268]
...
1841.01 0.46 PE L1384 MATMUL gp<-sh,w13h 128*88 128x512 f32 x1 [2.46 <-DVE hid L1268]
```

The others stand behind VectorE's operations of 2.89, 2.86 and 2.15 us beside GpSimd's, as in [rows 6].

**The clock was counted once.** I gave 1.5 us for the stop at step 2 and called chunk 0's 8.3 us of pauses, at a clock of 1.00, a sign that it does not fall there. In the changed kernel the clock was at its lower level behind the stop (2 us), behind chunk 0's pause (about 3.5: it was busy for some 7 us at half the clock there, and half of that is lost) and, in chunk 1, behind one pause of only 2.23 us (2.9 us). A pause has a second price that can be larger than itself, and it is not the same each time. The table's 4.1 of chunk 1 is 2.9 of this and 1.2 of too short a wait.

**The reciprocal in the loop** was right in its kind and place: one wait per chunk at tile 10, 2.14 to 2.23 in place of 1.8. Beside it tile 9 waits 0.4, and a chunk without either, with all of TensorE's work, is 43.2 and not 42.5. The 1.3 of chunk 2 is the sum of these small ones.

**The strips** were right in kind, and their price was 0.08 too low. The prediction's 0.56 rests on a group whose cost took in the longer spacing behind it; counted in the same way a group costs 0.64 (1868.20 to 1869.30, less two products). Six of them are 0.5 of the 0.7 us by which TensorE's work in a chunk was set too low. The rest is in places where a tile's first product follows the wide ones of the tile before: spacings of 0.30 to 0.34 in place of 0.23. Rival B's 0.93 did not happen. Here the changeover seen in the low-rank group [rows 4] was the better guide than the factor of 3.07 that the Trainium skill (TensorE: Matmul & The Clock Gate, Measured speedup vs the span model) gives four row tiles. That would be 0.30 a group, and the trace has 0.53 even without the spacing behind it.

**The 42 loads** were right in place and size: 0.30 us each, a stop of 6.51 for 7.0, and 8.6 with the clock for 8.5. Rivals A and D did not happen.

**Rival C happened in part.** GpSimd's additions held the casts, which have one input from SBUF, to 2.54 and 1.88 us. But five of 16 casts were held and not all, and a hold to 1.88 fits into a step, so it cost 2.2 us and not 20, and 2.4 more came from VectorE's own pieces. My 1.0 counted on 1.8 us of idleness a step and set pieces "up to 2.8 us" beside it without asking which steps also split contents. The Trainium skill (GPSIMD Engine Reference, Specifications) names operations in a 2-port mode among those that GpSimd contends with, and the trace agrees so far: the cast is held, though it has one input. In which mode it runs, no row here shows.

## What to carry to other kernels

When a change replaces a direct load by store, landing and reload, follow that chain to its first reader in the first round, with the queue's other entries ahead of it, before any bound is taken from the old wait. Price a new pause of TensorE twice: for itself, and for what half a clock may take behind it, 1 to 4 us here, or nothing. Work of an engine off the critical path belongs where it has time (13.4 us of reciprocals in the y stage were free, 3.3 in the loop cost 2.2 and more), and merging it to save its total was no gain here.

## What the runs showed of the hardware

- Behind a pause of 2.23 us TensorE's granted clock was 0.5 for some 6 us in one chunk and stayed 1.00 in the next, in the same execution. Which pauses are followed by it changed from run to run.
- Four products of 12 rows in four row strips start within 0.01 us and cost 0.53 together, and two cost 0.51; with the longer spacing behind them it is 0.64 and 0.62.
- A fp32r cast of 64 x 1024 took 0.69 us alone and 2.54 beside GpSimd's cast of keys and an addition of 1.30. Two masking operations of 128 x 256 took 0.34 and 0.48 alone, and 0.85 and 1.46 beside two additions.
- Loads of two partitions and up to 2.7 KB left the queue every 0.30 us, 42 in a row as well as two.
- In the run with the outputs ahead of the spread reciprocals, 2 MB of both, issued between 1804.8 and 1810.3, were complete only at 1819.2.
